# Ranks of the chosen experts in bfloat16, and the chain up to the gathered rows cut into other pieces, in a rotation and mixture-of-experts kernel

## The reference, cut to what matters

```python
x_right   = hamilton(filtered(x), conj(normalize(q_right)))   # rotation of each row's four quarters
x_rotated = hamilton(normalize(q_left), x_right)              # q_left is cond_256
logits = x_rotated.reshape(4096, 512) @ gate_w.T              # 8 experts
scores = softmax(logits); topv, topi = top_k(scores, 2)
gates  = topv / sum(topv)
loc    = rank of the token among those that chose the same expert (first choices, then second choices)
valid  = loc < 1024                                           # capacity of an expert
h      = relu(einsum('ecd,ehd->ech', dispatched, fc1_w) + fc1_b)   # fc1_w: 8 x 2048 x 512
eo     = einsum('ech,ehd->ecd', h, fc2_w) + fc2_b
out    = x + sum over both choices of eo[expert, loc] * gate * valid
```

## Time and profile before

| | |
|---|---|
| median of 3 runs | 1415.31 us (1414.93 to 1415.47) |
| the profiled execution, its own time | 1415.69 us |
| its span in the trace | 1413.7 us |
| mean granted TensorE clock | 0.99 |
| PE busy | 1378.0 us, 97% of the span |
| DVE busy | 1053.3 us, 75% |
| ACT busy | 705.0 us, 50% |
| POOL busy | 314.6 us, 22% |
| DMA | 194.41 MB, 138 GB/s in the mean |

### The profile page before, as it was taken

How to read it: one execution, slowest core, us unless ns; L and a number is a source line. 1 busy time by engine, 2 the same in 40 slices (tenths; PEclk the granted TensorE clock), 3 DMA queues, 4 the chain that set the end, 5 groups by cost and what they waited for, 6 DMA issues and landing times.

```text
span 1413.7 us, 18054 instructions
## 1 busy us (share of the span) xinstructions
PE 1378.0 (97%) x6175; PEld 1131.0 (80%) x6175; DVE 1053.3 (75%) x1582; ACT 705.0 (50%) x1058; POOL 314.6 (22%) x333
## 2 busy tenths in 40 slices
PE   8679999999999999999999999999999999999997
PEld 6458888888888888888888888888888888888885
DVE  6898779687877778687886878687796868865443
ACT  5456455544555445455464455454455454644442
POOL 1174203320125103221034202241032200220021
PEclk9799999999999999999999999999999999999998
DMA  8677666656457555566466565575465533543232
GB/s 286 252 175 180 131 129 178 156 115 140 106 164 172 133 99 157 150 133 146 88 187 164 106 136 133 144 162 137 90 179 148 110 75 67 156 119 69 52 104 74
DMA packets 449676, 194.41 MB, mean 138 GB/s; under 512 B 398464, under 2 KB 401673, under 8 KB 447794
## 3 DMA queue, kind: packets, MB, share of 16 engines
q1 hardware_dynamic: 427378, 125.98, 40.5%
q0 software_dynamic: 22208, 67.29, 15.3%
HBM read 153.47 MB, written 39.98 MB: 137 GB/s over the span
## 4 chain that ended last, share of the span: by engine, by line
PE 95%; DVE 3%; DMA 1%; issue 1%; ACT 0%; SPq 0%; POOL 0%; POOLq 0%
PE ps L1253 15%; PE ps L1257 15%; PE ps L1263 15%; PE ps L1228 14%; PE ps L1229 14%; PE ps L1230 14%; PE ps L1171 1%; PE ps L1244 1%; PE ps L1245 1%; PE ps L1246 1%; DVE yfull L958 1%; PE ps L1151 1%; PE ps L1152 1%; DMA x_all<-in_x 0%; DVE yfull L971 0%
## 5 line engine op out<-in xcount | busy, mean ns | idle before, releaser
L1228 PE MATMUL ps<-yc_hi,w1c_hi 128*128 128x512 f32 x896 | 349.5, 390 | 1.2 <-DVE yc_lo L924 1.2
L1230 PE MATMUL ps<-yc_hi,w1c_lo 128*128 128x512 f32 x896 | 348.7, 389 | 0.0
L1229 PE MATMUL ps<-yc_lo,w1c_hi 128*128 128x512 f32 x896 | 348.6, 389 | 0.0
L1253 PE MATMUL ps<-w_hi,h_hi 128*128 128x512 f32 x952 | 254.4, 389 | 0.0
L1257 PE MATMUL ps<-w_hi,h_lo 128*128 128x512 f32 x952 | 254.4, 389 | 0.0
L1263 PE MATMUL ps<-w_lo,h_hi 128*128 128x512 f32 x952 | 254.4, 389 | 0.0
L1263 PEld LDWEIGHTS ps<-w_lo,h_hi 128*128 128x128 f32 x952 | 178.7, 188 | 37.2
L1253 PEld LDWEIGHTS ps<-w_hi,h_hi 128*128 128x128 f32 x952 | 178.7, 188 | 37.1
L1257 PEld LDWEIGHTS ps<-w_hi,h_lo 128*128 128x128 f32 x952 | 178.7, 188 | 37.0
L1228 PEld LDWEIGHTS ps<-yc_hi,w1c_hi 128*128 128x128 f32 x896 | 168.1, 188 | 39.2 <-DVE yc_lo L924 2.2
L1230 PEld LDWEIGHTS ps<-yc_hi,w1c_lo 128*128 128x128 f32 x896 | 168.2, 188 | 35.3
(11 more groups left out here) (182 smaller groups left out, 1506.4 us busy)
## 6 DMA issues: line engine op xcount, KB each, us to landing
w_raw<-in_L_ffn_fc_w SPq DMA_DIRECT2D x232, 256.0 KB, 3.0
w_raw<-in_L_ffn_fc_w SPq DMA_DIRECT2D x512, 64.0 KB
slots_dram<-x_blk POOLq DMA_DIRECT2D x28, 512.0 KB, 3.8
x_blk<-slots_dram SPq DMA_DIRECT2D x224, 64.0 KB, 2.6
out<-x_all SPq DMA_DIRECT2D x8, 1024.0 KB, 13.0
x_all<-in_x SPq DMA_DIRECT2D x6, 1024.0 KB, 13.7
b_bc<-in_L_ffn_fc_b POOLq DMA_DIRECT2D x8, 256.0 KB, 3.8
x_all<-in_x SPq DMA_DIRECT2D x4, 256.0 KB, 3.8
```

Of the source, the lines that this page charges most:

```text
L1228: pe.matmul(bank, hi, yc_hi[:, y, q, :], start=first and q == 0, stop=False, skip_group_check=True)
L1229: pe.matmul(bank, hi, yc_lo[:, y, q, :], start=False, stop=False, skip_group_check=True)
L1230: ins = pe.matmul(bank, lo, yc_hi[:, y, q, :], start=False, stop=last and q == 1, skip_group_check=True)
L1253: pe.matmul(eo_s[:, b, :], h_hi[:, c, blk], w2_hi[:, w, :], start=False, stop=False, skip_group_check=True)
```

## The change

It does six things. The four transposes of `turn_logits` become four float32 matmuls by a 16x8 matrix `both_parts` (two identities on top of each other), which turn the logits and add their two parts; `both_parts` is one addition on POOL, and the addition on DVE goes. The products with `first_f` and their maxima go to bfloat16. The scan is made once for each choice, the first of them before the second choice is looked for, and the counts of earlier partitions come in three matmuls, two for the first choice and one for the second. The tables of slots are made in five parts of 16, 16, 16, 8 and 8 tiles. SP waits for all eight blocks of gathered rows before it issues `load_w1(2)`. `w1_low_parts(1, 0)` goes ahead of `rotate_ps(0)`, and T3's low part ahead of `y_sum(0, 3)`.

```diff
+    PARTS = ((0, 0, JH), (0, JH, TJ), (1, 0, JH), (1, JH, TJ - JH // 2), (1, TJ - JH // 2, TJ))
...
             load_w1(1)
+
+            for arrived in x0_in:
+                sp.wait_ge(arrived, 16)
             load_w1(2)
...
+            pool.wait_ge(consts_ready, 1)
+            pool.tensor_tensor(both_parts[:, :], ident[0:2 * E, 0:E], ident[0:2 * E, E:2 * E], ALU.add)
...
             dve.wait_ge(logits_T, CHUNKS)
-            link(dve.tensor_reduce(lg[:, :, :], logits_hl.rearrange("p j a e -> p j e a"), X, ALU.add))
...
-                link(dve.tensor_tensor(wt[:, :, :], from_, per_e(v), ALU.is_equal))
-                link(dve.tensor_tensor(wt[:, :, :], wt[:, :, :], first_bc, ALU.mult))
-                link(dve.reduce_max(w, wt[:, :, :], X))
-                link(dve.tensor_tensor(hot_k, wt[:, :, :], per_e(w), ALU.is_equal))
+                link(dve.tensor_tensor(wt_bf, from_, per_e(v), ALU.is_equal))
+                link(dve.tensor_tensor(wt_bf, wt_bf, first_bc, ALU.mult))
+                link(dve.reduce_max(w, wt_bf, X))
+                link(dve.tensor_tensor(hot_k, wt_bf, per_e(w), ALU.is_equal))
...
-            dve.wait_ge(consts_ready, 3)
-            dve.tensor_tensor_scan(cnt[:, :, :].rearrange("p k j -> p (k j)"),
...
+                    dve.wait_ge(consts_ready, 3)
+                dve.tensor_tensor_scan(cnt[:, k * E:(k + 1) * E, :].rearrange("p e j -> p (e j)"),
...
-            dve.wait_ge(ahead_ready, 1)
-            link(dve.tensor_tensor(cnt[:, :, :], cnt[:, :, :], ahead_ps.unsqueeze(2).to_broadcast([P, TOPK * E, TJ]), ALU.add))
-            link(dve.tensor_tensor(loc[:, :, :], cnt[:, :, :], hot3, ALU.mult))
+            dve.tensor_scalar(base_kj[:, :, :], chosen[:, :, :], -float(APART), float(E * APART), ALU.mult, ALU.add)
+            for k in range(TOPK):
+                of_k = slice(k * E, (k + 1) * E)
+                dve.wait_ge(ahead_ready, k + 1)
+                link(dve.tensor_tensor(cnt[:, of_k, :], cnt[:, of_k, :], ahead_ps[k].unsqueeze(2).to_broadcast([P, E, TJ]), ALU.add))
+                ins = dve.tensor_tensor(loc[:, of_k, :], cnt[:, of_k, :], hot[:, k, :, :], ALU.mult)
+            link(ins)
...
-            for c in range(2 * TOPK):
...
+            for c, (k, begin, end) in enumerate(PARTS):
+                js, pairs, m = slice(begin, end), slice(begin // 2, end // 2), (end - begin) // 2
...
+            w1_low_parts(1, 0)
             rotate_ps(0)
-            w1_low_parts(1, 0)
             rotate_ps(1)
...
             y_low(0, T1, t1)
+            y_low(0, T3, y12)
             y_sum(0, 3)
-            y_low(0, T3, y12)
             y_low(0, T4, y21)
...
-                    at = (g * XC + t) * 2 * E
-                    ins = pe.transpose(xp_all[:, at:at + 2 * E], logitsT[:, g % 2, t * P:(t + 1) * P],
-                                       ident[0:2 * E, 0:2 * E])
+                    at = (g * XC + t) * E
+                    ins = pe.matmul(xp_all[:, at:at + E], logitsT[:, g % 2, t * P:(t + 1) * P], both_parts[:, :],
+                                    start=True, stop=True)
...
             pe.wait_ge(counts_ready, 1)
-            pe.matmul(ahead_ps, before[:, :], cnt[:, :, TJ - 1], start=True, stop=False)
-            pe.matmul(ahead_ps[:, E:2 * E], ones[:, :], cnt[:, 0:E, TJ - 1], start=False, stop=True).then_inc(ahead_ready, 1)
+            pe.matmul(ahead_ps[1], ones[:, :], cnt[:, 0:E, TJ - 1], start=True, stop=False)
+            pe.matmul(ahead_ps[0], before[:, :], cnt[:, 0:E, TJ - 1], start=True, stop=True).then_inc(ahead_ready, 1)
+            pe.wait_ge(counts_ready, 2)
+            pe.matmul(ahead_ps[1], before[:, :], cnt[:, E:2 * E, TJ - 1], start=False, stop=True).then_inc(ahead_ready, 1)
```

More of the change, by code:

```diff
@@ L122, in program @@
         grot_hl = sb("grot_hl", [P, Q, 2 * E], F32R, where=early)
-        lg = sb("lg", [P, TJ, E], where=early)
+        both_parts = sb("both_parts", [2 * E, E], where=early)
         j1 = sb("j1", [P, TJ], BF16, where=early)
@@ L127, in program @@
         first_i = sb("first_i", [P, E], I32, where=early)
-        first_f = sb("first_f", [P, E], where=early)
+        first_f = sb("first_f", [P, E], BF16, where=early)
+        chosen = sb("chosen", [P, TOPK, TJ], BF16, where=early)
         spaced = sb("spaced", [P, BLOCKS, 2], BF16, where=early)
@@ L185, in program @@
         xth = ps[:, :, :].rearrange("p a (b n) -> p (a b) n", b=2)
-        logits_hl = xp_all.rearrange("p (j a e) -> p j a e", a=2, e=E)
-        ahead_ps = hp[:, 0, 0:TOPK * E]
+        logits_ps = xp_all[:, 0:TJ * E].rearrange("p (j e) -> p j e", e=E)
+        ahead_ps = [hp[:, k, 0:E] for k in range(TOPK)]
         token_ps = hp[:, 0, 0:2 * BLOCKS].rearrange("p (a q) -> p a q", a=2)
@@ L534, in _ @@
             act.wait_ge(part_ready, 1)
-            for c in range(2 * TOPK):
-                k, pairs = c // 2, slice(c % 2 * JH // 2, (c % 2 + 1) * JH // 2)
+            for c, (k, begin, end) in enumerate(PARTS):
                 act.wait_ge(hot_t_ready, c + 1)
-                act.activation(hot_q[:, k, pairs, 1, :, :], hot_t[:, c % 2, :, :, :], ACT.Copy, scale=part_f[:, :]
+                act.activation(hot_q[:, k, begin // 2:end // 2, 1, :, :], hot_t[:, c % 2, 0:(end - begin) // 2, :, :], ACT.Copy,
+                               scale=part_f[:, :]
                                ).then_inc(hots_p_ready, 1)
@@ L847, in _, with of_pairs @@
             link(dve.scalar_tensor_tensor(b_f[:, :, :], block_f[:, :, :], -float(P), place[:, :, :], ALU.mult, ALU.add))
-            def of_pairs(ap, width):
-                return ap.rearrange("p (m t) -> p m t", t=2).unsqueeze(2).to_broadcast([P, JH // 2, width, 2])
-            for c in range(2 * TOPK):
-                k, js = c // 2, slice(c % 2 * JH, (c % 2 + 1) * JH)
-                pairs = slice(c % 2 * JH // 2, (c % 2 + 1) * JH // 2)
-                numbers = value[:, :, :].unsqueeze(1).to_broadcast([P, JH // 2, P, 2])
+            for c, (k, begin, end) in enumerate(PARTS):
+                js, pairs, m = slice(begin, end), slice(begin // 2, end // 2), (end - begin) // 2
+                def of_pairs(ap, width):
+                    return ap.rearrange("p (m t) -> p m t", t=2).unsqueeze(2).to_broadcast([P, m, width, 2])
+                numbers = value[:, :, :].unsqueeze(1).to_broadcast([P, m, P, 2])
+                blocks = spaced[:, :, :].unsqueeze(1).to_broadcast([P, m, BLOCKS, 2])
+                table = hot_t[:, c % 2, 0:m, :, :]
                 if c >= 2:
@@ L1198, in _ @@
             idle(12)
-            for c in range(2 * TOPK):
+            for c, (k, begin, end) in enumerate(PARTS):
                 pe.wait_ge(hots_ready, c + 1)
                 pe.wait_ge(hots_p_ready, c + 1)
-                for j in range(c % 2 * JH, (c % 2 + 1) * JH):
-                    ins = pe.matmul(token_ps, hot_b[:, c // 2, j // 2, :, j % 2], hot_q[:, c // 2, j // 2, :, :, j % 2],
-                                    start=(c == 0 and j == 0), stop=(c == 2 * TOPK - 1 and j == TJ - 1))
+                for j in range(begin, end):
+                    ins = pe.matmul(token_ps, hot_b[:, k, j // 2, :, j % 2], hot_q[:, k, j // 2, :, :, j % 2],
+                                    start=(c == 0 and j == 0), stop=(c == len(PARTS) - 1 and j == TJ - 1))
                 ins.then_inc(hots_used, 1)
```

27 lines of the change are left out of this document (12 added, 15 removed).

## The result

The changed kernel takes 1417.35 us (median of 20 runs, 1416.24 to 1418.20), and the kernel before 1415.51 us (20 runs, 1413.97 to 1417.17). The ratio is 1.0012, with a 95% interval from 1.0006 to 1.0017: 1.84 us more, 0.1%. The prediction was 1416.7 us, from 1413.0 to 1419.6, and "within 0.2%" had most of the chance. It held. The changed kernel is a little slower, by less than the 0.2% that I had set as the smallest difference to be told. The profiled execution took 1417.64 us, with a span of 1415.8; the one before had 1415.69 and 1413.7.

What follows compares the result with a forecast made beforehand. PE bounds the unchanged steady state; only the start of p6 of group 1 moves. +3.9 - 0.94 - 0.83 - 0.62 - 0.97 + 0.85 = +1.4 on the profiled 1415.69, median 0.4 lower: 1416.7 us, range 1413.0 to 1419.6.

Steps and rivals of the forecast that it cites:

- within 0.2%: Whole kernel: the forecast case that the time differs by under 0.2%, 2.8 us, from the kernel before; chance 0.67.
- Step 1: PE's eight turns of the logits: float32 matmuls as two pieces each, 0.105 us a piece, all on the chain: +3.9 us.
- rival of dearer turns: PE's eight turns: 0.21 us a piece instead of 0.105, +10.6 us, 1423.4 us in all; deciding from 0.128; chance 0.15.
- Steps 2 and 3: DVE's choice of experts, -0.94 us (addition gone, bfloat16 product, split scan), and counts of earlier partitions, -0.83 us.
- Step 4: Slot tables in five parts: PE's last burst halves to 8 matmuls, -0.82, DVE's extra instructions +0.2: -0.62 us.
- Step 5: First gathered rows: moving `w1_low_parts(1, 0)` into DVE's wait -0.87, SP's wait making the second gather earlier -0.1: -0.97 us.
- earlier second gather: First gathered rows: without the transfers of `load_w1(2)` beside it, the second gather lands perhaps 0.1 us earlier: -0.1.
- the wait before the rotation: DVE before `rotate_ps(0)`: a sign of being right was that this wait, 1.74 us before, shrinks below 1.
- PE's diagonal products would come forward: PE after the gathers: later gathers land up to 2 us earlier, which keeps PE's slack of 1.16 from being eaten.
- Step 6: T3's low part before T4's sum: ACT's high parts run later, delaying p6 of group 1 from 107.81 to 108.66, +0.85 us.
- PE's expected wait of 0.4: PE before p3 or p6 of group 1: a wait of some 0.4 us ended by DVE would show the prediction right.
- The rival in which T3 gains: T3's low part moved ahead: p7's wait of 0.4 us goes and B22's delay finds slack, 1415.4 us; chance 0.15.

## Why the prediction was right

**Step 1, the turns: mechanism right, size off.** Two pieces an instruction, and every chunk on the path: so it was. The term was too small. I had halved the 0.21 of half clock: 0.105 a piece was predicted and 0.123 measured, +5.1 instead of +3.9. This is the mis-sized term of the sum. The rival of dearer turns had the right direction, but its 0.21 a piece was far off. It was to decide from 0.128 a piece on. The Trainium skill (FP8 and Floating Point Precision, TensorE Precision Notes) gives true float32 four passes; the x64 for 32 instructions shows two pieces each at this shape, so the estimate of 16 pieces a chunk came out too high as well: there were eight. Two things brought the sum back: this profile's logits had started 0.76 earlier than those of the profile before, by the arrival of x, and over all profiles the old turn loses some 0.5 to DVE's transposes, which the new one does not. Neither stood in the prediction.

**Steps 2 and 3, choice and counts: right.** -1.78 against -1.77. PSUM costs nothing more here: 0.42 both ways, so the Trainium skill's 120 against 58 cycles (VectorE: DVE Perf Modes, The TRN2 errata) does not show in these rows. The maxima over bfloat16 stayed at 0.42, the scan's half took the 0.69 that I had worked out, and PE's matmul for the second choice was ready 0.16 ahead of DVE's need, where 0.2 was predicted.

**Step 4, five parts: right,** -0.75 against -0.62. What I did not see is that it hangs on the clock: at full clock it is worth 0.2.

**Step 5, rotation and SP: the move right, the rest not.** Moving `w1_low_parts(1, 0)` gave -0.85 against -0.87. The other -0.1 was to come from an earlier second gather. That landed 0.28 earlier, but PE's clock fell behind its waits for the first rows, and the turn of the second block took 0.46 longer: +0.18 in all. The other profiles show the same two parts. With the clock held, the rotation begins 7.90 to 7.99 behind `j_part` with SP's wait and 8.16 to 8.21 without; where it fell, 8.11 to 8.42 with it and 8.66 to 8.77 without. So the term of the clock was missing from the prediction, and the wait before the rotation stayed at 1.05, where below 1 was to be its sign. I had also said that PE's diagonal products would come forward. They did, from 9.61 behind the rotation's start to 8.80, though they waited 1.89 for ACT's `x_turned`; but they took 8.63 instead of 7.07, with the clock at 0.69 and 0.80 in the windows from 85 to 92. So PE's slack of 1.16 at the third sum was gone, and its matmuls there began 0.3 later behind the sum than before (1.65 instead of 1.36). That cost nothing up to p6 of group 1: two kernels whose PE waited there have the same 11.99 and 11.98. Why ACT was late in this execution stays open; its copy began at 85.39 after 3.24 of idle time, though the two blocks that it reads had been turned by 83.4, and the kernels with the turn alone and with the added matmuls show waits of 2.8 to 3.5 there too.

**Step 6, T3: right,** +0.76 against +0.85, by the chain that was predicted: ACT's high parts later, p4 later by 0.25 (8.63 behind the third sum instead of 8.38), L800 later by 1.0. PE's expected wait of 0.4 before p3 or p6 came in two parts too short for a bracket: from p4's last third to p3 and from p3's to p6 of group 1 the starts lie 0.2 and 0.3 further apart than before. The rival in which T3 gains falls: the traces at full clock separate the two orders without overlap. What I did not see is that this term, too, hangs on the clock: in the four profiles that compare where it fell at the third sum, 12.12 with T3 ahead and 12.06 to 12.20 with T3 behind, T3's place costs nothing that shows.

**The sum.** With what the traces show, 5.12 - 1.78 - 0.75 - 0.67 + 0.76 = +2.7 from one first turn to the same point; with the mean over all profiles, 4.66 in place of 5.12, it is +2.2. Measured are 1.84, from 0.8 to 2.4. The predicted +1.4 was near because five of the six terms held to 0.3; the sixth was too low, by 0.8 on the mean of the profiles and by 1.2 between the profile before and the one after. That the median still came within 0.7 of the forecast is in part luck: the turns cost less in the medians than between these two profiles, and nothing in the prediction said so. The best versions, with the old turn, stand at 0.9983 to 0.9989, which is 1.6 to 2.4 us under the kernel before and 3 to 4 under the changed one. They can't be told from each other. T3 back is worth its 0.76 in the traces at full clock only.

## What to carry to other kernels

A small float32 matmul that replaces a transpose costs PE a weight load for each of its two pieces (here 0.98 us for four instead of 0.35); where PE has no idle time, count the pieces, and don't move a 0.7 us addition off DVE by adding 0.6 us to PE eight times. When an operation moves ahead of a sum, follow the sum's other reader (here ACT), not only the low part that gets ready sooner. A profile is one execution: where engines run neck and neck, compare the same stretch in several profiles before a term below 1 us is called a gain.
